# Attention on one core: where the value products and the work on the shared PSUM bank stand inside a unit

## The chip, the cores and the metric

The kernel runs on one core of a Trainium2 chip. It is one program with three stages: a feed-forward block, an attention block, a second feed-forward block. The metric is the time of one execution in microseconds of device time, as the median of several runs. The change touches only the order of work in the attention stage.

## What is computed

The input has 16 batches of 512 rows of 128 numbers. A row is first passed through a feed-forward block (a mixture of experts plus a shared part), then through attention with 16 heads of 8 numbers, then through the feed-forward block again, each on a normalised input and with a residual. The attention part is the one that matters here:

```python
x = x + 0.5 * _L0_ffn_ref(_layernorm(x, axis=-1), ...)
x = x + _L0_attn_ref(_layernorm(x, axis=-1), ...)
x = x + 0.5 * _L0_ffn_ref(_layernorm(x, axis=-1), ...)

def _L0_attn_ref(x, Wq, bq, Wk, bk, Wv, bv, Wo, bo, head_mask):
    q = (x @ Wq.T + bq).reshape(b, s, HEADS, HEAD_DIM)
    k = (x @ Wk.T + bk).reshape(b, s, HEADS, HEAD_DIM)
    v = (x @ Wv.T + bv).reshape(b, s, HEADS, HEAD_DIM)
    attn = jnp.einsum('bqhd,bkhd->bhqk', q, k) / np.sqrt(HEAD_DIM).astype(np.float32)
    attn = jax.nn.softmax(attn, axis=-1)
    attn = attn * head_mask[None, :, None, None]
    out = jnp.einsum('bhqk,bkhd->bqhd', attn, v).reshape(b, s, HIDDEN)
    return out @ Wo.T + bo
```

## The kernel before

`attention` handles the 16 batches one after another. A batch is 16 **units** (u = 0 to 15): four groups of four heads (a "quad") times four tiles of 128 keys. A unit has two halves, each for two heads of its quad. In a half TensorE (PE) makes two things, each into a bank pair of a ring of three (`p_score`):

- `score_exp`, line 927, two matmuls: the scores of this unit, from which ScalarE (ACT) makes the exponentials (line 1096);
- `score_max`, line 941, two matmuls: the scores, the other way round, of the unit 8 units ahead, of which VectorE (DVE) takes the row maxima (line 1259).

I call them E0 and M0 for the first half and E1 and M1 for the second. The ring of three sets who waits for whom (`bank_free`): an M writes into the bank pair of the E one half earlier, so it waits until ACT has read that E; an E writes into the pair of the M two halves earlier, so it waits for DVE.

`times_values` (line 958) multiplies the exponentials of a unit with the values: four matmuls, which the trace shows as eight records, each on 32 of the array's columns, into the bank `p_o`. One tile of keys after another is summed there, and after every fourth unit ACT copies `p_o` out (`copy_o`, line 1102).

All other TensorE work of the attention goes through one more PSUM bank, `p_x`. I call each such step a **piece**. There are 14 in a batch, named in `X_USES`: the transposed maxima `m0` to `m3` (line 967), which a DMA then puts beside the queries before the quad's first E may run; the transposed outputs `o0` to `o3` (975); `norm` (982), `out` (988) and `v` (915); `x` (901); and `q` and `k` (907 to 909) of the batch after the next. Every piece fills `p_x` and waits until ACT or DVE has emptied it of the piece before (`x_bank_drained`).

The order of each engine's instructions is written by hand, in the functions `batch` and `pieces` of each engine. TensorE's order in a unit before the change is E0, M0, the unit's piece, E1, M1, value products of the unit before. In units 0 and 15 there is no piece. The engines run down their own lists and meet only at semaphores.

Of the kernel before, what the change touches and what calls it, by code (L numbers as in the profile page):

```python
# [101 lines left out]
def every_batch(eng, batch):  # L102

    for k in range(NB):
        batch(Turn(0, k), k == 0, k == NB - 1)
# [637 lines left out]
def attention(nc, w, src, dst):  # L743


    UNITS = NQ * NT
# [6 lines left out]
    with ExitStack() as ctx:  # L753
# [44 lines left out]
        def there(b, n=0):  # L798

            return not isinstance(b.j, int) or b.k + n < NB  # L800
# [93 lines left out]
        def _(pe):  # L894
# [97 lines left out]
            def batch(b, is_first, is_last):  # L992
                a, c = b.step(-1), b.step(1)
                for u in range(UNITS):
                    if u % NT == 0:
                        g = u // NT
                        pe.wait_ge(max_packed[g % 2], b.count(MAX_DMA * NQ // 2, MAX_DMA * (g // 2 + 1)))
                    ahead, v = (b, u + AHEAD) if u + AHEAD < UNITS else (c, u + AHEAD - UNITS)
                    if v == 0 and there(ahead):
                        pe.wait_ge(packed[ahead.par], ahead.half(PACK_DMA, PACK_DMA))  # L1000
                    for half in range(2):
                        score_exp(b, u, half)
                        if there(ahead):
                            score_max(ahead, v, half)
                        if half == 0:
                            pieces(b, u, is_first)
                        elif u > 0:
                            times_values(b, u - 1)
                        elif not is_first:
                            times_values(a, UNITS - 1)  # L1010

            def pieces(b, u, is_first):
                a, c, e = b.step(-1), b.step(1), b.step(2)
                if u == 1:
                    turn_max(b, 1, uses(b, "m1"))
                if not is_first:
                    if u == 2:
                        turn_o(a, 3, uses(b, "o3"))
                    if u == 3:
                        turn_norm(uses(b, "norm"))  # L1020
                    if u == 4:
                        project_out(uses(b, "out"))
                if u == 5:
                    turn_max(b, 2, uses(b, "m2"))
                if u == 6:
                    turn_o(b, 0, uses(b, "o0"))
                if u == 7 and there(c):
                    project_v(uses(b, "v"))
                if u == 8 and there(e):
                    turn_x(e, uses(b, "x"))  # L1030
                if u == 9:
                    turn_max(b, 3, uses(b, "m3"))
                if u == 10:
                    turn_o(b, 1, uses(b, "o1"))
                if u == 11 and there(e):
                    project_qk(e, w.wq, uses(b, "q"))
                if u == 12 and there(e):
                    project_qk(e, w.wk, uses(b, "k"))
                if u == 13 and there(c):
                    turn_max(c, 0, uses(b, "m0"))  # L1040
                if u == 14:
                    turn_o(b, 2, uses(b, "o2"))

            begin, end = Turn(0, 0), Turn(0, NB - 1)
# [20 lines left out]
        def _(act):  # L1065
# [48 lines left out]
            def pieces(b, u, half, is_first):  # L1114
                a, c, e = b.step(-1), b.step(1), b.step(2)
                now = (u, half)
                if now == (1, 0) and not is_first:
                    copy_o(a, 3, uses(a, "o1") + 1)
                if now == (1, 1):
                    copy_max(b, 1, uses(b, "m1"))  # L1120
                if now == (3, 1) and not is_first:
# [3 lines left out]
                if now == (5, 1):  # L1125
                    copy_max(b, 2, uses(b, "m2"))
                if now == (8, 1) and there(e):
                    x_copy(e, uses(b, "x"))
                if now == (9, 0):
                    copy_o(b, 1, 0 if is_first else uses(b, "o3") + 1)  # L1130
                if now == (9, 1):
                    copy_max(b, 3, uses(b, "m3"))
                if now == (10, 0) and there(e):
                    x_high(e, uses(b, "x"))
                if now == (11, 1) and there(e):
                    operand(e, "q", w.bq, uses(b, "q"))
                if now == (12, 0) and there(e):
                    operand_high(e, "q", uses(b, "q"))
                if now == (12, 1) and there(e):
                    operand(e, "k", w.bk, uses(b, "k"))  # L1140
                if now == (13, 0):
                    copy_o(b, 2, uses(b, "o0") + 1)
                if now == (13, 1) and there(c):
                    copy_max(c, 0, uses(b, "m0"))
                if now == (14, 0) and there(e):
                    operand_high(e, "k", uses(b, "k"))

            begin, end = Turn(0, 0), Turn(0, NB - 1)
            for n in range(2):
# [96 lines left out]
        def _(dve):  # L1246
# [49 lines left out]
            def pieces(b, now, is_first):  # L1296
                a, c, e = b.step(-1), b.step(1), b.step(2)
                if there(e):
                    if now == (2, 0):
                        norm_stats(e)  # L1300
                    if now == (3, 0):
                        norm_var(e)
                if not is_first:
                    if now == (2, 1):
                        normalise(a, NQ - 1, uses(b, "o3"))
                    if now == (4, 1):
# [3 lines left out]
                if now == (7, 1) and there(c):  # L1310
                    copy_values(c, uses(b, "v"))
                if now == (10, 1):
                    normalise(b, 1, uses(b, "o1"))
                if now == (14, 1):
                    normalise(b, 2, uses(b, "o2"))

            begin, end = Turn(0, 0), Turn(0, NB - 1)
# [83 lines left out]
```

## Time and profile before

| What | Value |
|---|---|
| Time, median of 3 runs | 2092.17 us (2088.86 to 2097.89) |
| The profiled execution | 2100.33 us, of it the span of the trace 2098.1 us |
| Busy share of the span | PE 89%, DVE 71%, ACT 59%, POOL 42% |
| First feed-forward block and start of attention | 0 to 647.4 us |
| First 15 batches of attention | 647.4 to 1471.1 us |
| Last batch of attention | 1471.1 to about 1520 us |
| Second feed-forward block | to 2098.1 us |
| Mean granted clock of TensorE, as a share of 2.4 GHz | 0.93 |

The trace is one execution. Times in it count from the start of the span, and the granted clock of a stretch is a mean: 1.00 is 2.4 GHz throughout, 0.50 is 1.2 GHz throughout.

### The profile page before, as it was taken

Reading aid. Unit: us, or ns where it says so; the run is one execution under the profiler, and the core shown is the slowest. Engines: PE = TensorE matmul, PEld = TensorE weight load, DVE = VectorE, ACT = ScalarE, POOL = GpSimd, SP = SyncE. Lnnn points to the kernel's source line nnn. Section 1 sums busy time; section 2 is a strip of 40 time slices with the busy share of each in tenths; the row PEclk is TensorE's granted clock in tenths of the full one; section 3 lists DMA queues with packets and bytes.
Section 4 is the critical chain, followed back from the end, with each engine's and each line's share of the span. In section 5 each row is a group of like instructions: output and inputs, shape, how many; then the busy total and the mean of one; then the engine's idle time right before and its main releaser. Section 6 shows DMA issues by size and latency. Waiting matters only on the chain. (4 is left out here: it accounts for less than half of the span.)

```text
span 2098.1 us, 30450 instructions
## 1 busy us (share of the span) xinstructions
PE 1860.1 (89%) x9600; PEld 1108.9 (53%) x9600; DVE 1496.2 (71%) x2379; ACT 1232.2 (59%) x1914; POOL 887.4 (42%) x875
## 2 busy tenths in 40 slices
PE   3999999999937898999999988888859999999999
PEld 2777777777812333333333333333247777777777
DVE  4767777687517878777787777887447768776775
ACT  3566455555513767666676667776635565556654
POOL 2566555655621222222222222221125565556655
PEclk9999999999955989888888889998879999999999
DMA  2000000000032323222223223222010000000000
GB/s 91 21 11 31 27 24 30 10 30 10 16 59 33 47 47 47 47 42 39 41 44 44 41 41 40 53 44 35 12 36 21 31 11 31 20 30 10 30 14 16
DMA packets 43167, 68.57 MB, mean 33 GB/s; under 512 B 9916, under 2 KB 11444, under 8 KB 43060
## 3 DMA queue, kind: packets, MB, share of 16 engines
q1 hardware_dynamic: 38256, 65.15, 15.7%
q0 software_dynamic: 4096, 1.08, 0.3%
q8 instruction: 58, 0.95, 0.2%
q10 hardware_dynamic: 708, 0.98, 0.1%
q14 instruction: 49, 0.40, 0.1%
HBM read 28.36 MB, written 12.58 MB: 20 GB/s over the span
## 5 line engine op out<-in xcount | busy, mean ns | idle before, releaser
L1259 DVE TENSOR_REDUCE attn_neg_max<-attn_p_score 128x2 f32<-128x1024 f32 x512 | 624.8, 1223 | 211.2 <-PE attn_p_score L941 209.1
L572 POOL TENSOR_TENSOR ffn_hid_low<-ffn_hidden,ffn_hid_high 128x512 fp32r<-128x512 f32 x448 | 580.6, 1298 | 454.9 <-ACT ffn_hid_high L512 454.2
L1096 ACT ACTIVATE attn_exps<-attn_p_score 128x1024 f32<-128x1024 f32 x512 | 519.8, 1025 | 286.6 <-PE attn_p_score L927 284.6
L512 ACT ACTIVATE ffn_hid_high<-ffn_hidden 128x512 fp32r<-128x512 f32 x448 | 281.0, 627 | 255.7 <-DVE ffn_hidden L705 254.8
L503 ACT ACTIVATE ffn_silu<-ffn_p_gate 128x512 f32<-128x512 f32 x448 | 264.0, 589 | 207.8 <-PE ffn_p_gate L375 207.5
L698 DVE TENSOR_TENSOR ffn_gated<-ffn_silu,ffn_p_up 128x512 f32<-128x512 f32 x352 | 240.6, 684 | 175.1 <-PE ffn_p_up L375 112.2
L941 PE MATMUL attn_p_score<-k_pack,q_pack 24*128 24x512 f32 x1024 | 283.2, 553 | 57.7 <-ACT attn_exps L1096 33.0
L958 PE MATMUL attn_p_o<-attn_exps,values 128*32 128x512 f32 x2048 | 312.0, 684 | 8.4 <-ACT attn_o_raw L1102 3.3
L927 PE MATMUL attn_p_score<-q_pack,k_pack 26*128 26x512 f32 x1024 | 271.2, 539 | 14.9 <-DMA q_pack<-attn_max_rows 14.6
L927 PEld LDWEIGHTS attn_p_score<-q_pack,k_pack 26*128 26x128 f32 x1024 | 101.4, 198 | 314.7 <-issue 207.5
L705 DVE TENSOR_TENSOR ffn_hidden<-ffn_gated,ffn_p_spread 128x512 f32<-128x512 f32 x352 | 241.2, 685 | 14.9 <-PE ffn_p_spread L416 4.1
L373 PE MATMUL ffn_p_y<-ffn_hid_high,down_high 128*128 128x512 f32 x448 | 186.3, 416 | 34.0 <-POOL ffn_hid_low L572 33.3
L373 PE MATMUL ffn_p_gate<-ffn_xt_high,gate_high 128*128 128x512 f32 x448 | 188.5, 421 | 0.0
L1203 POOL DMA_DIRECT2D q_pack<-attn_max_rows x128 | 74.3, 582 | 265.0 <-ACT attn_max_rows L1090 265.0
L373 PE MATMUL ffn_p_up<-ffn_xt_high,up_high 128*128 128x512 f32 x448 | 180.4, 403 | 2.9 <-DVE ffn_gated L698 2.8
L375 PE MATMUL ffn_p_up<-ffn_xt_low,up_high 128*128 128x512 f32 x448 | 177.5, 396 | 0.0
L375 PE MATMUL ffn_p_gate<-ffn_xt_low,gate_high 128*128 128x512 f32 x448 | 177.2, 396 | 0.0
L375 PE MATMUL ffn_p_y<-ffn_hid_low,down_high 128*128 128x512 f32 x448 | 177.1, 395 | 0.0
L374 PE MATMUL ffn_p_gate<-ffn_xt_high,gate_low 128*128 128x512 f32 x448 | 176.7, 394 | 0.0
L374 PE MATMUL ffn_p_up<-ffn_xt_high,up_low 128*128 128x512 f32 x448 | 176.2, 393 | 0.0
L374 PE MATMUL ffn_p_y<-ffn_hid_high,down_low 128*128 128x512 f32 x448 | 175.4, 391 | 0.0
L941 PEld LDWEIGHTS attn_p_score<-k_pack,q_pack 24*128 24x128 f32 x1024 | 103.9, 201 | 114.9 <-ACT attn_exps L1096 90.6
(146 smaller groups left out, 2220.9 us busy)
## 6 DMA issues: line engine op xcount, KB each, us to landing
q_pack<-attn_q_high SPq DMA_DIRECT2D x128, 64.0 KB
k_pack<-attn_k_high SPq DMA_DIRECT2D x128, 64.0 KB
ffn_x_in<-in_x SPq DMA_DIRECT2D x16, 256.0 KB, 2.8
ffn_x_res<-in_x SPq DMA_DIRECT2D x16, 256.0 KB, 2.8
after_ffn<-ffn_x_out SPq DMA_DIRECT2D x16, 256.0 KB, 2.0
attn_x_in<-after_ffn SPq DMA_DIRECT2D x16, 256.0 KB, 4.6
k_pack<-attn_k_low SPq DMA_DIRECT2D x64, 64.0 KB
q_pack<-attn_q_low SPq DMA_DIRECT2D x64, 64.0 KB
```

Source lines behind the costliest of these rows:

```text
L373: nc.tensor.matmul(out, weights[0], high, start=start, stop=False)
L374: nc.tensor.matmul(out, weights[1], high, start=False, stop=False)
L375: return nc.tensor.matmul(out, weights[0], low, start=False, stop=stop)
L503: nc.scalar.activation(silu[f % 2][0:n, :], p_gate[f % 2][0:n, :], ACT.Silu).then_inc(silu_ready, 1)
L512: nc.scalar.activation(hid_high[s][0:n, :], hidden[s][0:n, :], ACT.Copy).then_inc(high_ready, 1)
L572: nc.gpsimd.tensor_tensor(hid_low[s][0:n, :], hidden[s][0:n, :], hid_high[s][0:n, :].bitcast(F32), ALU.subtract).then_inc(low_ready, 1)
L705: V.tensor_tensor(hidden[slot(b, f)][:], gated[f % 2][:], p_spread[:], ALU.mult).then_inc(weighted_ready, 1)
L927: last = nc.tensor.matmul(score_bank("exp", b, n)[:, i, :], pack["k"][b.par][rows, g, t * P:(t + 1) * P], pack["q"][b.par][rows, g, :], st ...
L941: last = nc.tensor.matmul(score_bank("max", b, n)[:, j % 2, :], pack["q"][b.par][rows, g, t * P:(t + 1) * P], pack["k"][b.par][rows, g, :] ...
L958: last = nc.tensor.matmul(p_o[h * COLS:(h + 1) * COLS, :], values[b.par][:, t, g * QUAD + h, :], exps[(2 * u + h // 2) % len(exps)][:, h % ...
L1096: nc.scalar.activation(exps[n % len(exps)][:], score_bank("exp", b, n)[:], ACT.Exp, scale=inv_sqrt)\
L1259: V.tensor_reduce(neg_max[g % 2][:, j:j + 2, t], score_bank("max", b, n)[:], AX.X, ALU.max, negate=True).then_inc(max_read, 1)
```

## The change

On TensorE the value products of two units now stand together. At the end of each even unit u come those of units u-2 and u-1, sixteen records in a row; at the end of an odd unit there are none. The piece, which stood between the two halves, now stands after everything else of a unit, and each piece comes one unit number earlier: the piece of unit 5 before is now that of unit 4. ACT's and DVE's steps on `p_x` and `p_o` are moved to match, mostly to the first half of the unit after the piece. Nothing is added or taken away.

```diff
                         score_exp(b, u, half)
                         if there(ahead):
                             score_max(ahead, v, half)
-                        if half == 0:
-                            pieces(b, u, is_first)
-                        elif u > 0:
-                            times_values(b, u - 1)
-                        elif not is_first:
-                            times_values(a, UNITS - 1)
+                    if u % 2 == 0:
+                        for back in (2, 1):
+                            if u > 0:
+                                times_values(b, u - back)
+                            elif not is_first:
+                                times_values(a, UNITS - back)
+                    pieces(b, u, is_first)
...
-                if u == 1:
+                if u == 0:
                     turn_max(b, 1, uses(b, "m1"))
...
-                if u == 5:
-                    turn_max(b, 2, uses(b, "m2"))
-                if u == 6:
+                if u == 5:
                     turn_o(b, 0, uses(b, "o0"))
...
             every_batch(pe, batch)
+            times_values(end, UNITS - 2)
             times_values(end, UNITS - 1)
...
-                if now == (1, 0) and not is_first:
-                    copy_o(a, 3, uses(a, "o1") + 1)
-                if now == (1, 1):
+                if now == (1, 0):
+                    if not is_first:
+                        copy_o(a, 3, uses(a, "o1") + 1)
                     copy_max(b, 1, uses(b, "m1"))
...
-                if now == (6, 1):
+                if now == (6, 0):
                     normalise(b, 0, uses(b, "o0"))
```

On TensorE, in a batch in the middle, from unit 3 into unit 5. Before:

```order
L927 MATMUL attn_p_score<-q_pack,k_pack 128x512 x2
L941 MATMUL attn_p_score<-k_pack,q_pack 128x512 x2
L982 MATMUL attn_p_x<-ident,attn_o_norm 128x128 x4
L927 MATMUL attn_p_score<-q_pack,k_pack 128x512 x2
L941 MATMUL attn_p_score<-k_pack,q_pack 128x512 x2
L958 MATMUL attn_p_o<-attn_exps,values 32x512 x4
L927 MATMUL attn_p_score<-q_pack,k_pack 128x512 x2
L941 MATMUL attn_p_score<-k_pack,q_pack 128x512 x2
L988 MATMUL attn_p_x<-wo,attn_ot 128x128 x4
```

TensorE again, the same place after the change, units 3 and 4:

```order
L927 MATMUL attn_p_score<-q_pack,k_pack 128x512 x2
L941 MATMUL attn_p_score<-k_pack,q_pack 128x512 x2
L927 MATMUL attn_p_score<-q_pack,k_pack 128x512 x2
L941 MATMUL attn_p_score<-k_pack,q_pack 128x512 x2
L988 MATMUL attn_p_x<-wo,attn_ot 128x128 x4
L927 MATMUL attn_p_score<-q_pack,k_pack 128x512 x2
L941 MATMUL attn_p_score<-k_pack,q_pack 128x512 x2
L927 MATMUL attn_p_score<-q_pack,k_pack 128x512 x2
L941 MATMUL attn_p_score<-k_pack,q_pack 128x512 x2
L958 MATMUL attn_p_o<-attn_exps,values 32x512 x8
L967 MATMUL attn_p_x<-ident,attn_max_parts 32x128
```

The piece is gone from between the halves; E0, M0, E1 and M1 follow each other in every unit, and the value products come every second unit, eight matmuls at a time.

On ScalarE, units 5 and 6 of such a batch. Before:

```order
L1102 ACTIVATE attn_o_raw<-attn_p_o 128x512
L1096 ACTIVATE attn_exps<-attn_p_score 128x1024
L1090 ACTIVATE attn_max_rows<-attn_p_x 32x128
L1096 ACTIVATE attn_exps<-attn_p_score 128x1024 x6
L1069 ACTIVATE attn_xt<-attn_p_x 128x512
```

ScalarE after the change, the same place:

```order
L1104 ACTIVATE attn_o_raw<-attn_p_o 128x512
L1092 ACTIVATE attn_max_rows<-attn_p_x 32x128
L1098 ACTIVATE attn_exps<-attn_p_score 128x1024 x6
L1071 ACTIVATE attn_xt<-attn_p_x 128x512
```

The two copies now stand together between the exponentials of unit 5's first and second half.

## Rows read from the trace of the kernel before

**Rows 1.** Busy time by stretch: microseconds, busy time (and records) of each engine, clock, DMA:

```profile
647.40:1471.10 823.70, 736.80 (x4556) 275.45 (x4556) 642.76 (x781) 561.74 (x697) 210.43 (x337) 0.89 0.27 42
1471.10:1520.00 48.90, 42.93 (x259) 14.51 (x255) 22.43 (x26) 33.32 (x40) 6.02 (x13) 0.83 0.02 8
...
1312.60:1363.70 51.10, 44.64 (x310) 17.22 (x306) 42.96 (x54) 37.72 (x47) 14.53 (x23) 1.00 0.28 49
```

**Rows 2.** TensorE in order of time, units 14 and 15: start, length, line, count, idle before:

```profile
1027.10 0.50 PE L927 MATMUL attn_p_score<-q_pack,k_pack 26*128 26x512 f32 x2
...
1027.54 0.66 PE L975 MATMUL attn_p_x<-ident,attn_o_raw 128*128 128x128 f32 x4
1028.12 0.50 PE L927 MATMUL attn_p_score<-q_pack,k_pack 26*128 26x512 f32 x2
1028.72 0.50 PE L941 MATMUL attn_p_score<-k_pack,q_pack 24*128 24x512 f32 x2
1029.15 1.06 PE L958 MATMUL attn_p_o<-attn_exps,values 128*32 128x512 f32 x8
1030.15 0.50 PE L927 MATMUL attn_p_score<-q_pack,k_pack 26*128 26x512 f32 x2
...
1030.54 0.50 PE L927 MATMUL attn_p_score<-q_pack,k_pack 26*128 26x512 f32 x2
1031.76 0.52 PE L941 MATMUL attn_p_score<-k_pack,q_pack 24*128 24x512 f32 x2 [0.72 <-ACT attn_exps L1096]
```

**Rows 3.** ScalarE in order of time, the exponentials of unit 15:

```profile
1030.69 1.94 ACT L1096 ACTIVATE attn_exps<-attn_p_score 128x1024 f32<-128x1024 f32 x2 [0.59 <-PE attn_p_score L927]
```

**Rows 4.** TensorE in order of time, the same batch boundary at the lower clock:

```profile
1032.21 1.94 PE L958 MATMUL attn_p_o<-attn_exps,values 128*32 128x512 f32 x8
1034.08 0.79 PE L927 MATMUL attn_p_score<-q_pack,k_pack 26*128 26x512 f32 x2
...
1035.99 0.79 PE L941 MATMUL attn_p_score<-k_pack,q_pack 24*128 24x512 f32 x2 [0.69 <-ACT attn_exps L1096]
1036.71 1.93 PE L958 MATMUL attn_p_o<-attn_exps,values 128*32 128x512 f32 x8
1038.58 0.79 PE L927 MATMUL attn_p_score<-q_pack,k_pack 26*128 26x512 f32 x2
```

**Rows 5.** Busy time by stretch around a fall and a rise of the clock:

```profile
1030.50:1032.10 1.60, 0.88 (x8) 0.37 (x4) 1.56 (x3) 1.41 (x2) 0.05 (x1) 1.00 0.02 5
1032.10:1049.10 17.00, 16.24 (x71) 4.99 (x69) 10.36 (x15) 7.75 (x10) 1.58 (x4) 0.50 0.57 80
1161.80:1165.20 3.40, 3.40 (x20) 2.01 (x20) 1.90 (x2) 1.69 (x2) 1.01 (x3) 0.50 0.54 63
1165.20:1169.00 3.80, 3.30 (x29) 0.94 (x21) 3.40 (x4) 2.76 (x5) 1.27 (x1) 1.00 0.78 140
```

**Rows 6.** Pieces on TensorE in order of time, at the upper clock:

```profile
1018.40 0.47 PE L907 MATMUL attn_p_x<-attn_xt_high,wq_high 128*128 128x512 f32 x1 [0.47 <-DVE attn_o_norm L1277]
...
1018.94 0.39 PE L909 MATMUL attn_p_x<-attn_xt_low,wq_high 128*128 128x512 f32 x1
...
1024.71 0.27 PE L967 MATMUL attn_p_x<-ident,attn_max_parts 128*32 128x128 f32 x1 [0.17 <-ACT attn_k_full L1079]
...
1488.23 1.16 PE L988 MATMUL attn_p_x<-wo,attn_ot 128*128 128x128 f32 x8
```

**Rows 7.** Pieces on TensorE in order of time, at the lower clock:

```profile
1039.31 0.40 PE L967 MATMUL attn_p_x<-ident,attn_max_parts 128*32 128x128 f32 x1
...
1043.81 1.11 PE L975 MATMUL attn_p_x<-ident,attn_o_raw 128*128 128x128 f32 x4
...
1161.54 2.08 PE L988 MATMUL attn_p_x<-wo,attn_ot 128*128 128x128 f32 x8
```

**Rows 8.** Waits between 650 and 1500 us: total, times, longest:

```profile
PE attn_p_score L927 <- DMA q_pack<-attn_max_rows: 11.2, 7, 3.2
```

More of the change, by code:

```diff
@@ L1019, in pieces @@
                     if u == 3:
-                        turn_norm(uses(b, "norm"))
-                    if u == 4:
                         project_out(uses(b, "out"))
+                if u == 4:
+                    turn_max(b, 2, uses(b, "m2"))
                 if u == 5:
-                    turn_max(b, 2, uses(b, "m2"))
-                if u == 6:
                     turn_o(b, 0, uses(b, "o0"))
-                if u == 7 and there(c):
+                if u == 6 and there(c):
                     project_v(uses(b, "v"))
-                if u == 8 and there(e):
+                if u == 7 and there(e):
@@ L1030, in pieces @@
                     turn_x(e, uses(b, "x"))
+                if u == 8:
+                    turn_max(b, 3, uses(b, "m3"))
                 if u == 9:
-                    turn_max(b, 3, uses(b, "m3"))
-                if u == 10:
                     turn_o(b, 1, uses(b, "o1"))
+                if u == 10 and there(e):
+                    project_qk(e, w.wq, uses(b, "q"))
                 if u == 11 and there(e):
-                    project_qk(e, w.wq, uses(b, "q"))
-                if u == 12 and there(e):
@@ L1038, in pieces @@
                     project_qk(e, w.wk, uses(b, "k"))
-                if u == 13 and there(c):
+                if u == 12 and there(c):
                     turn_max(c, 0, uses(b, "m0"))
-                if u == 14:
+                if u == 13:
                     turn_o(b, 2, uses(b, "o2"))
@@ L1116, in pieces @@
                 now = (u, half)
-                if now == (1, 0) and not is_first:
-                    copy_o(a, 3, uses(a, "o1") + 1)
-                if now == (1, 1):
+                if now == (1, 0):
+                    if not is_first:
+                        copy_o(a, 3, uses(a, "o1") + 1)
                     copy_max(b, 1, uses(b, "m1"))
-                if now == (3, 1) and not is_first:
+                if now == (3, 0) and not is_first:
                     copy_ot(uses(b, "norm"))
@@ L1124, in pieces @@
                     copy_o(b, 0, 0 if is_first else uses(a, "o2") + 1)
[L1125 removed]
                     copy_max(b, 2, uses(b, "m2"))
+                if now == (8, 0) and there(e):
+                    x_copy(e, uses(b, "x"))
                 if now == (8, 1) and there(e):
[L1128 removed]
+                    x_high(e, uses(b, "x"))
                 if now == (9, 0):
                     copy_o(b, 1, 0 if is_first else uses(b, "o3") + 1)
[L1131 removed]
                     copy_max(b, 3, uses(b, "m3"))
[L1133 to L1134 removed]
+                if now == (11, 0) and there(e):
+                    operand(e, "q", w.bq, uses(b, "q"))
                 if now == (11, 1) and there(e):
[L1136 removed]
+                    operand_high(e, "q", uses(b, "q"))
                 if now == (12, 0) and there(e):
[L1138 removed]
+                    operand(e, "k", w.bk, uses(b, "k"))
                 if now == (12, 1) and there(e):
[L1140 removed]
+                    operand_high(e, "k", uses(b, "k"))
                 if now == (13, 0):
                     copy_o(b, 2, uses(b, "o0") + 1)
[L1143 to L1146, printed above, removed]
+                    if there(c):
+                        copy_max(c, 0, uses(b, "m0"))
             begin, end = Turn(0, 0), Turn(0, NB - 1)
@@ L1298, in pieces @@
                 if there(e):
-                    if now == (2, 0):
+                    if now == (1, 0):
                         norm_stats(e)
-                    if now == (3, 0):
+                    if now == (2, 1):
                         norm_var(e)
                 if not is_first:
-                    if now == (2, 1):
+                    if now == (2, 0):
                         normalise(a, NQ - 1, uses(b, "o3"))
-                    if now == (4, 1):
+                    if now == (4, 0):
                         residual(a, uses(b, "out"))
-                if now == (6, 1):
+                if now == (6, 0):
                     normalise(b, 0, uses(b, "o0"))
-                if now == (7, 1) and there(c):
+                if now == (7, 0) and there(c):
                     copy_values(c, uses(b, "v"))
-                if now == (10, 1):
+                if now == (10, 0):
                     normalise(b, 1, uses(b, "o1"))
-                if now == (14, 1):
+                if now == (14, 0):
                     normalise(b, 2, uses(b, "o2"))
```

4 lines of the change are left out of this document (3 added, 1 removed).

## The prediction, made before the changed kernel had run

> **What bounds the kernel now.** I read the busy time by stretch first, since the change touches only the attention. The first 15 batches take 823.7 us, 54.9 us each, and the last one 48.9 us. TensorE is busy 736.8 of the 823.7 us, more than DVE (642.8) or ACT (561.7), and its mean granted clock there is 0.89. One batch, from 1312.6 to 1363.7 us, ran at 1.00 throughout and took 51.1 us [rows 1]. So two things make up a batch: TensorE's own order of work, and the time it spends at its lower clock.
>
> Then I read TensorE in order of time. Unit 14 has a piece. It starts at 1027.10; the piece (the output transposes) runs from 1027.54 to 1028.12; E1 follows, M1 starts at 1028.72, the value products at 1029.15, and the next unit at 1030.15: 3.05 us. Unit 15 has no piece. It starts at 1030.15, E1 stands at 1030.54, and then TensorE idles 0.72 us until M1 at 1031.76, released by ACT [rows 2]. The reason stands in ACT's rows: the exponential of E0 starts at 1030.69, and two together take 1.94 us, so the first leaves at about 1031.7 [rows 3]. M1 needs that bank pair. **M1 comes 1.61 us after E0 whether or not there is a piece between them.** That is the cover under which pieces run today. At the lower clock the same distance is 1035.99 - 1034.08 = 1.91 us [rows 4].
>
> **The change at the upper clock.** With the piece behind M1 a unit is, to the start of the next thing, 1.61 (E0 to M1) + 0.43 (M1) + 1.00 (value products, here as half of a double block) = 3.04 us [rows 2], and the piece comes on top. Sixteen units are 48.6 us. Pieces, from start to the next score (a row's length less 0.07, as 1027.54 + 0.66 against 1028.12): turning maxima 0.20; four transposes 0.59; `out` and `v` 1.09 each; `q` and `k` 0.86 each, from 1018.40 to 1018.94 + 0.39 [rows 2, 6]. A batch has 4, 6, 2 and 2 of these: 0.80 + 3.54 + 2.18 + 1.72 = 8.2 us. Together 56.9 us, against 51.1 for the batch of before at that clock. The unit's end gives them no cover: TensorE runs in order and nobody else is late there.
>
> **The same at the lower clock.** A unit is 1.91 + 0.72 (M1 to the value products) + 1.87 (value products, 1036.71 to 1038.58) = 4.50 us [rows 4], sixteen are 72.0. Pieces: 0.33, 1.04, 2.01 [rows 7], and for `q` and `k`, which no row shows at this clock in a steady batch, between 0.86 and twice that, 1.72; I take 1.55, 0.86 scaled as the transposes are (1.04 to 0.59). Sum 1.32 + 6.24 + 4.02 + 3.10 = 14.7. A batch is 86.7 us.
>
> **Which clock.** The falls of before show when it goes. After the 1.6 us of units 14 and 15 in which TensorE was busy 0.88, without any piece, the clock stood at 0.50 for 17 us [rows 5]. Unit 15 before that fall had eight records of value products, the scores, one wait of 0.72 and no piece. In the steady batches the falls come in units 15 and 0, the two without a piece, or where TensorE waits for a DMA in front of unit 4. The rises are the other way round: from 1161.8 to 1165.2 us TensorE was busy all 3.40 us, most of it with the projection of `out` (2.08 us, full array, [rows 7]) and value products, and after it the clock was 1.00 [rows 5]. Fully busy stretches of mostly scores did not lift it: the 17 us at 0.50 were 16.24 busy.
>
> The changed order makes both happen in every pair of units. Between two blocks of value products stand the piece, the scores of an odd unit with their wait, a second piece and the scores of an even unit with their wait: at the upper clock 0.59 + 2.04 + 0.59 + 2.04 = 5.3 us with no value products in them and two waits of 0.7, leaner than units 15 and 0 were. So I expect the clock to fall there. Then come sixteen records of value products and a piece without a wait, 3.74 + 1.04 = 4.8 us at the lower clock, denser than what lifted the clock before. So I expect it to rise behind them, too late for the block itself. **The clock is low in the even unit, the block and its piece, and high in the odd unit.** Per pair: scores of the even unit 1.91 + 0.72 = 2.63; block 2 x 1.87 = 3.74; scores of the odd unit 1.61 + 0.43 = 2.04; 8.41 us, eight pairs 67.3. Pieces after even units (four times 0.33, `norm` 1.04, `v` 2.01, `q` 1.55) 5.9; after odd ones (five times 0.59, `out` 1.09, `k` 0.86) 4.9. A batch is 78.1 us.
>
> The Trainium skill says otherwise ("TensorE: Matmul & The Clock Gate", section "Why this matters for your kernels"): it ties a throttled clock to pauses between bursts of matmuls several times longer than any here. By that rule the clock would stay up. The trace speaks against it, since the clock fell behind a wait of 0.72 us; I keep it as the third case below.
>
> **Smaller terms.** The wait of E for the maxima's DMA, 11.2 us in seven [rows 8], goes: the piece `m1` comes a unit earlier and the units are longer. It is in the 54.9 of before and not in my 78.1. The two ACT copies that now stand together delay the exponential of an odd unit's second half, and so M0 of the next unit, by up to 0.6 us, four times a batch. But the following M1 has to wait 1.61 us after E0 anyway, and swallows it. I take 0; if it didn't, up to 1.2 us a batch, 18 in all. DVE's steps are moved by half a unit; DVE has 22% of the stretch free [rows 1], 0. Changes between score matmuls, value products and full-array work fall from eight to five per pair. What one costs is bounded by the value block: 1.00 us at the upper clock where half of 1.87 is 0.935, so 0.065 at most from that side, 24 times a batch 1.6 us, 25 in all; below, nothing. I take 0, since most of it is hidden behind running matmuls.
>
> "TensorEngine Tiling (Array Packing)" in the Trainium skill, section "Key Properties", says that a change of tiling mode drains TensorE, which speaks for this change. It gives no price; with the bound just worked out the sum would be 25 us lower.
>
> **The sum.** 78.1 - 54.9 = 23.2 us for 15 batches, 348. The last batch has look-ahead scores only in its first half: half of 23.2 there, 12, and nothing in the second half. Together 360 us. The profiled execution took 2100.3, so its like would take 2460; it stood 8 us above the median of the runs, and 2092 + 360 gives **2452 us**.
>
> **Rivals.**
>
> *Lower clock throughout.* If the blocks don't lift the clock (no row shows sixteen records in a row), a batch is 86.7: 31.8 x 15 + 16 = 493, 2585 us. For it: fully busy stretches that didn't lift it. Against it: those were mostly scores.
>
> *Lower clock for a third.* If it falls more rarely, say every second or third pair, a batch is 56.9 + 29.8 / 3 = 66.8: 11.9 x 15 + 6 = 185, 2277 us. For it: one whole batch of before kept 1.00 [rows 1]. Against it: that batch had cover for its pieces.
>
> *Upper clock throughout, and slightly slower.* 56.9 - 54.9 = 2.0 x 15 + 1 = 31, 2123 us; with the 25 of the mode changes 2098.
>
> *Faster.* The denser blocks keep the clock up, and a mode change costs more than my bound. The batch then gives back 54.9 - 51.1 = 3.8 us of low clock and loses 5.8 to uncovered pieces. It breaks even at 2.0 / 24 = 0.083 us per change saved. At 0.15 a batch is 1.6 us shorter, 2092 - 24 = 2068 us. Against it: the clock fell at a leaner density of waits than the new order has.
>
> **Chances.** Alternating clock 66%; lower throughout 14%; a third 12%; upper throughout 8%, of it 3 faster, 2 the same, 3 slower. I call "the same" a time within 0.5% of 2092, about what a measurement here can tell. The range reaches from the case of a third to that of the lower clock throughout: 2280 to 2590. The likeliest case alone would lie between 2400 and 2500. Faster 0.03, same 0.02, slower 0.95.
>
> **What would show it.** In the trace of the changed kernel, M1 1.6 us behind E0 at the upper and 1.9 at the lower clock in every unit, with TensorE idle about 0.7 before it, released by ACT: right. M1 earlier than that: my first step is wrong. Sixteen records of value products that take 3.7 us, with scores of the odd unit 0.5 us long: alternating clock, mean granted clock in the attention about 0.64 (low for 8 x 6.37 + 5.9 = 56.9 of 78.1 us). A mean near 0.5 or 0.95 is one of the rivals. Pieces with idle time before them, waiting for the bank, or E waiting for the maxima's DMA, would be a term that I left out. The feed-forward stages should keep their time.

## The result, and the profile after

The changed kernel took 2423.76 us (median of 4 runs, 2418.72 to 2424.01), the kernel before 2095.03 us with them. The ratio is 1.157, with a 95% interval of 1.153 to 1.160: 329 us slower. Ratios here leave out executions that took over 1.5% longer than the fastest of the same kernel. The forecast was 360 us slower, 2452 us, with a range of 2280 to 2590.

The busy time by stretch of the changed kernel (microseconds, then busy time and records of PE, weight loads, DVE, ACT and POOL, then clock and DMA), to be read against [rows 1]:

```profile
648.30:1784.80 1136.50, 959.32 (x4550) 348.77 (x4550) 641.45 (x780) 556.59 (x697) 210.25 (x337) 0.67 0.19 31
...
1254.80:1330.30 75.50, 63.50 (x308) 23.34 (x308) 43.00 (x53) 37.41 (x48) 14.51 (x23) 0.68 0.22 33
1176.80:1254.80 78.00, 66.17 (x308) 23.88 (x308) 43.14 (x53) 37.38 (x48) 14.51 (x23) 0.65 0.20 32
```

The first 15 batches grew from 823.7 to 1136.5 us, from 54.9 to 75.8 us each. DVE and ACT did the same work as before (642 and 557 us). The mean granted clock went from 0.89 to 0.67; since the trace has only the two levels 1.00 and 0.50, that is a share of 2 x (1 - 0.67) = 66% of the stretch at 1.2 GHz; before it was 22%. The feed-forward stages kept their time.

TensorE in order of time in the changed kernel, end of unit 4 to unit 8 of a batch (start, length, line, count, idle before), to be read against [rows 2, 4]:

```profile
1276.56 1.92 PE L958 MATMUL attn_p_o<-attn_exps,values 128*32 128x512 f32 x16
...
1278.63 0.50 PE L927 MATMUL attn_p_score<-q_pack,k_pack 26*128 26x512 f32 x2
...
1278.97 0.40 PE L927 MATMUL attn_p_score<-q_pack,k_pack 26*128 26x512 f32 x2
1280.24 0.50 PE L941 MATMUL attn_p_score<-k_pack,q_pack 24*128 24x512 f32 x2 [0.87 <-ACT attn_exps L1098]
1280.96 0.63 PE L975 MATMUL attn_p_x<-ident,attn_o_raw 128*128 128x128 f32 x4 [0.22 <-ACT attn_max_rows L1092]
1281.52 0.56 PE L927 MATMUL attn_p_score<-q_pack,k_pack 26*128 26x512 f32 x2
...
1283.19 0.79 PE L941 MATMUL attn_p_score<-k_pack,q_pack 24*128 24x512 f32 x2 [0.21 <-ACT attn_exps L1098]
1283.91 3.64 PE L958 MATMUL attn_p_o<-attn_exps,values 128*32 128x512 f32 x16
1287.48 1.70 PE L915 MATMUL attn_p_x<-wv,attn_xt 128*128 128x128 f32 x8
1289.12 0.49 PE L927 MATMUL attn_p_score<-q_pack,k_pack 26*128 26x512 f32 x2
...
1290.73 0.50 PE L941 MATMUL attn_p_score<-k_pack,q_pack 24*128 24x512 f32 x2 [0.87 <-ACT attn_exps L1098]
1291.57 0.68 PE L901 MATMUL attn_p_x<-ident,attn_xn 128*128 128x128 f32 x4 [0.35 <-DVE values L1265]
1292.18 0.79 PE L927 MATMUL attn_p_score<-q_pack,k_pack 26*128 26x512 f32 x2
...
1294.10 0.79 PE L941 MATMUL attn_p_score<-k_pack,q_pack 24*128 24x512 f32 x2 [0.60 <-ACT attn_exps L1098]
1294.82 3.64 PE L958 MATMUL attn_p_o<-attn_exps,values 128*32 128x512 f32 x16
```

Read the lengths. In unit 5 a pair of scores takes 0.50 us, so the clock is up; TensorE waits 0.87 us for ACT in front of M1, then runs the piece in the open. In unit 6 the scores turn to 0.79 us in mid-unit, and the sixteen records of value products take 3.57 us (1283.91 to 1287.48), at the lower clock. Behind them, in unit 7, the scores are back at 0.5. In unit 8 the low clock is there from the first score. The same in windows over that stretch:

```profile
1283.90:1287.40 3.50, 3.50 (x18) 0.60 (x16) 1.50 (x3) 0.15 (x1) 0.00 (x0) 0.50 0.00 0
1287.40:1289.10 1.70, 1.70 (x12) 1.51 (x8) 0.00 (x0) 0.00 (x0) 0.00 (x0) 0.63 0.00 0
1289.10:1292.10 3.00, 1.78 (x13) 0.91 (x12) 2.41 (x3) 1.94 (x2) 0.00 (x0) 0.99 0.00 0
1292.10:1298.70 6.60, 6.00 (x27) 1.56 (x25) 3.00 (x3) 2.94 (x4) 0.43 (x2) 0.50 0.01 2
```

TensorE's clock is low where it is busy all the time and high where it is busy 1.78 of 3.00 us: in this stretch the upper clock arrives when the dense work is over.

### The profile page after: what moved, and what is told of

It is laid out like the page before. It is cut to its first block and busy times, and to the rows that moved or that the text cites. A ratio compares the mean times of both kernels' runs of the same rounds, so it can differ in the third digit from the quotient of the medians.

```text
span 2421.8 us, 30419 instructions
## 1 busy us (share of the span) xinstructions
PE 2087.0 (86%) x9569; PEld 1184.4 (49%) x9600; DVE 1496.1 (62%) x2379; ACT 1227.2 (51%) x1914; POOL 887.4 (37%) x875
## 5 line engine op out<-in xcount | busy, mean ns | idle before, releaser
L1098 ACT ACTIVATE attn_exps<-attn_p_score 128x1024 f32<-128x1024 f32 x512 | 511.8, 1021 | 613.8 <-PE attn_p_score L927 611.6
L941 PE MATMUL attn_p_score<-k_pack,q_pack 24*128 24x512 f32 x1024 | 329.0, 643 | 170.5 <-ACT attn_exps L1098 153.9
L958 PE MATMUL attn_p_o<-attn_exps,values 128*32 128x512 f32 x2048 | 443.8, 1014 | 1.0 <-ACT attn_exps L1098 1.0
L927 PE MATMUL attn_p_score<-q_pack,k_pack 26*128 26x512 f32 x1024 | 260.8, 567 | 12.8 <-DVE attn_neg_max L1259 8.2
L941 PEld LDWEIGHTS attn_p_score<-k_pack,q_pack 24*128 24x128 f32 x1024 | 119.8, 232 | 298.6 <-ACT attn_exps L1098 271.8
L1194 POOL TENSOR_TENSOR attn_max_parts<-attn_neg_max,zeros 128x16 fp32r<-128x16 f32 x64 | 13.9, 218 | 494.7 <-DVE attn_neg_max L1259 494.7
L958 PEld LDWEIGHTS attn_p_o<-attn_exps,values 128*32 128x32 f32 x2048 | 73.7, 153 | 212.5 <-issue 145.1
```

The source lines that it names most:

```text
L927: last = nc.tensor.matmul(score_bank("exp", b, n)[:, i, :], pack["k"][b.par][rows, g, t * P:(t + 1) * P], pack["q"][b.par][rows, g, :], st ...
L941: last = nc.tensor.matmul(score_bank("max", b, n)[:, j % 2, :], pack["q"][b.par][rows, g, t * P:(t + 1) * P], pack["k"][b.par][rows, g, :] ...
L958: last = nc.tensor.matmul(p_o[h * COLS:(h + 1) * COLS, :], values[b.par][:, t, g * QUAD + h, :], exps[(2 * u + h // 2) % len(exps)][:, h % ...
L1098: nc.scalar.activation(exps[n % len(exps)][:], score_bank("exp", b, n)[:], ACT.Exp, scale=inv_sqrt)\
```

## The experiments

The theory (A) has two parts. The pieces lost their cover, the wait for M1; and the clock falls between the double blocks of value products and rises behind them. Its rivals put all of the loss on the first part (B), on the idle gap in each unit (C, I), or on the spacing of value products alone (E). Each run is compared with the kernel before on its own chip, whose median was between 2094 and 2101 us.

### Half of the change each

**Value products in pairs, pieces as before.**

```diff
                         if half == 0:
                             pieces(b, u, is_first)
-                        elif u > 0:
-                            times_values(b, u - 1)
-                        elif not is_first:
-                            times_values(a, UNITS - 1)
+                        elif u % 2 == 0:
+                            for back in (2, 1):
+                                if u > 0:
+                                    times_values(b, u - back)
+                                elif not is_first:
+                                    times_values(a, UNITS - back)
...
             every_batch(pe, batch)
+            times_values(end, UNITS - 2)
             times_values(end, UNITS - 1)
```

> The value products of two units stand together at each even unit's end, as in the changed kernel; the pieces keep their place between the two halves, as before. Theory A (two costs: uncovered pieces, and a clock that falls in the units without value products and rises behind each double block): the pieces are covered again, but the clock still alternates, so a batch falls from 75.8 us to about 8 x 8.4 + the overhang of the long pieces = 68 to 70 us, 2300 us in all, and the mean granted clock of the attention stays near 0.70. Rival B (all of the loss is the lost cover under M1): about 2095 us, as before, at a clock near 0.89.

Measured: 2249.78 us, ratio 1.070 (1.062 to 1.078), 149 us slower. Busy time by stretch, its first 15 batches:

```profile
647.90:1615.70 967.80, 847.09 (x4548) 319.86 (x4549) 642.20 (x780) 559.79 (x697) 210.32 (x337) 0.76 0.22 36
```

With every piece back under the wait the clock still alternates: 0.76, so 48% of the stretch is low. B is out. A batch takes 64.5 us, less than the 68 to 70 that I expected: 37 of the 128 double blocks took 1.85 us, all at the upper clock, and 38 took 3.57, against 11 and 111 in the changed kernel.

**Pieces at the end, value products of one unit in every unit.**

```diff
-                    if u % 2 == 0:
-                        for back in (2, 1):
-                            if u > 0:
-                                times_values(b, u - back)
-                            elif not is_first:
-                                times_values(a, UNITS - back)
+                    if u > 0:
+                        times_values(b, u - 1)
+                    elif not is_first:
+                        times_values(a, UNITS - 1)
                     pieces(b, u, is_first)
...
             every_batch(pe, batch)
-            times_values(end, UNITS - 2)
             times_values(end, UNITS - 1)
```

> The pieces and all copies stand where the changed kernel has them; the value products of one unit stand in each unit's end, as before, ahead of the piece. Theory A: every unit has its eight value records again, so the clock is up most of the time; a batch is 56.9 us at the upper clock and some 2 to 5 us more for low stretches around the two units without a piece, 57 to 62 us, 2130 to 2210 us in all, clock 0.88 or more. Rival B (all of the loss is the lost cover): near 2424 us. Rival C (the clock falls because each unit now has an idle wait of 0.7 us, wherever the value products stand): clock near 0.67 and 2400 us or more.

Measured: 2172.59 us, ratio 1.035 (1.025 to 1.044), 72 us slower. Busy time by stretch, the first 15 batches and one whole batch at the upper clock, and behind it two rows of TensorE:

```profile
647.30:1551.40 904.10, 700.76 (x4559) 258.47 (x4560) 643.36 (x781) 553.60 (x697) 210.58 (x337) 0.92 0.25 39
892.20:949.80 57.60, 43.72 (x310) 16.63 (x307) 43.05 (x54) 37.18 (x47) 14.53 (x23) 1.00 0.25 43
```

```profile
1085.96 0.50 PE L941 MATMUL attn_p_score<-k_pack,q_pack 24*128 24x512 f32 x2 [0.87 <-ACT attn_exps L1095]
...
1089.22 0.50 PE L941 MATMUL attn_p_score<-k_pack,q_pack 24*128 24x512 f32 x2 [0.79 <-ACT attn_exps L1095]
```

The second fence is TensorE in order of time, M1 of two units in a row: every unit now has a wait of 0.8 to 0.9 us before M1, and TensorE is busy 700.76 of 904.1 us (78%), less than in the changed kernel (84%; part of that is only that the same matmuls last longer at the lower clock). Yet the clock is at 0.92. So C is out: idle gaps of this size don't take the clock down where every unit has its value products. The batch at 1.00 takes 57.6 us; the lost cover costs 57.6 - 51.1 [rows 1] = 6.5 us a batch at equal clock.

The two halves cost 149 and 72 us, together 221, and the whole change 329. The missing 108 us are the two acting on each other, and most of it by the clock: by length and mean clock the 15 batches spend about 180 us at the lower clock before, 465 and 145 in the two halves, and 750 in the changed kernel, some 320 more than the halves add up to. My reading is that the wait which the pieces no longer fill makes the stretch between the blocks emptier, and that a piece in the open costs about twice as much at the lower clock ([rows 6, 7]: 1.16 and 2.08 us for eight records). No run separates these two.

### Work added to the changed kernel

**Four, then eight, useless transposes in each unit's wait.** They go into the bank pair that E1 overwrites right behind them.

```diff
+            def filler(b, u, times):
+                bank_free(pe, "exp", b, 2 * u + 1)
+                for n in range(times):
+                    for t in range(NT):
+                        nc.tensor.transpose(score_bank("exp", b, 2 * u + 1)[:, n % 2, t * P:(t + 1) * P], w.ident[:], w.ident[:])
...
                         if there(ahead):
                             score_max(ahead, v, half)
+                        if half == 0:
+                            filler(b, u, 1)
```

> The changed kernel with useless work added: in every unit, between M0 and E1, four transposes of the identity into the bank pair that E1 overwrites right behind. E1 then starts at 1.0 instead of 0.4 us, still ahead of M1 at 1.6, so the filler itself is covered by the wait. Theory A (the low clock between the double blocks is the larger cost): the clock is up much more of the time, a batch goes from 75.8 to 58 to 64 us, 2150 to 2230 us in all, though work is added. Rival E (the clock follows the spacing of the value products alone, and filler does not count): 2424 us or slightly more, clock 0.67 in the attention.

> As the run before, with eight transposes, so that E1 starts at 1.5 us, still ahead of M1. Theory A: if four left some low stretches, eight leave next to none: the changed order at the upper clock, 57 to 59 us a batch, 2130 to 2160 us. That is what the uncovered pieces cost by themselves. Rival E: 2424 us or more.

Measured: 2192.14 us with four, ratio 1.047 (1.039 to 1.055), and 2169.42 us with eight, ratio 1.035 (1.028 to 1.041). Busy time by stretch, the 15 batches and one of them, with four and then with eight:

```profile
647.00:1558.50 911.50, 866.14 (x5508) 387.54 (x5508) 640.78 (x780) 565.09 (x697) 211.27 (x337) 0.94 0.24 38
1132.40:1190.50 58.10, 55.13 (x372) 25.54 (x371) 42.94 (x53) 38.03 (x48) 14.58 (x23) 1.00 0.29 43
```

```profile
647.50:1534.90 887.40, 854.13 (x6468) 471.05 (x6469) 642.96 (x780) 566.54 (x696) 210.94 (x337) 0.99 0.25 39
...
1003.90:1063.10 59.20, 57.05 (x438) 31.47 (x435) 43.09 (x53) 38.11 (x47) 14.56 (x23) 1.00 0.29 42
```

The run with eight settles it. The order of the changed kernel is untouched, 1920 transposes are added to its first 15 batches, and it is 254 us faster. The clock stays at 1.00 from the second of these batches to the last. E is out. Of the 329 us that the change costs, at least 254 go with the clock. The 75 that remain are not the price of the order alone: the kernel before also spent 22% of its attention at the lower clock, and the filler has a price of its own. At equal clock a batch takes 51.1 us before, 58.1 with four transposes and 59.2 with eight; by the 1.1 us between the last two I estimate 57 without any, 6 us a batch for the order.

**Score matmuls as filler.** The same place in each unit; E1's own two matmuls are made three extra times.

```diff
...
+                for _ in range(3):
+                    for i in range(2):
+                        nc.tensor.matmul(score_bank("exp", b, n)[:, i, :],
+                                         pack["k"][b.par][rows, g, t * P:(t + 1) * P],
+                                         pack["q"][b.par][rows, g, :], start=True, stop=True,
+                                         tile_position=((2 + i) * ROWS, 0))
```

> The changed kernel again with filler between M0 and E1 in every unit, but of the other kind: E1's own two score matmuls (32 of the array's rows each) are made three extra times, about 1.0 us, and overwritten. TensorE is then as busy in the wait as with eight full-array transposes. Rival I (what keeps the clock up is that TensorE does not idle): 2150 to 2190 us and a clock of the attention near 0.99, as with the eight transposes. Theory A2 (score matmuls count for less than full-array work and value products): the clock still alternates, 0.70 to 0.85, and the time lies between 2250 and 2430 us.

Measured: 2269.31 us (median of 4, 2214.8 to 2287.35). Busy time by stretch, of an execution of 2264 us, and behind it the filler of one unit and the E1 that follows:

```profile
647.00:1632.00 985.00, 925.79 (x6033) 429.65 (x6033) 646.82 (x785) 566.57 (x701) 211.49 (x341) 0.87 0.22 36
```

```profile
1108.39 0.86 PE L999 MATMUL attn_p_score<-q_pack,k_pack 26*128 26x512 f32 x6
1109.09 0.39 PE L927 MATMUL attn_p_score<-q_pack,k_pack 26*128 26x512 f32 x2
```

TensorE is busy 925.79 of 985.0 us, 94%, and the clock is at 0.87, against 0.99 with the transposes and 0.92 in the run that was busy only 78%. So I is out, too: it isn't idleness as such. The six filler matmuls took 0.70 us (1108.39 to 1109.09), not the 1.0 expected, so the fair comparison is with four transposes, 0.58 us: TensorE was then busy 866.14 of 911.5 us, 95%, and the clock was 0.94. Score matmuls helped, but less than full-array transposes over no more time. The median lies in the range of A2, the clock a little above it; even the fastest of the four, 2214.8 us, is slower than every run with transposes and outside the range of rival I. How much each kind counts was not measured one by one.

### The kernel before: can its own low stretches be had?

The same reasoning says that the kernel before loses time at its two empty units, 0 and 15. Seven runs followed it.

**Filler in units 0 and 15** (four transposes of the identity into `p_x` once it is drained).

> The kernel before, with useless work added: in the two units of a batch without a piece (0 and 15) four transposes of the identity into the shared bank, which nobody reads, between the two halves. Theory A: the filler is covered by the wait for M1 and keeps the clock up there, so the low stretches of 3.8 us worth a batch go: 2095 - 16 x 3.8 = about 2035 us, mean clock of the attention 0.97 or more. Rival C (the clock falls by the idle gap itself or for another reason): 2095 us or slightly more, the low stretches stay.

Measured: 2089.92 us, ratio 0.992 (0.987 to 0.996). The medians are 11 us apart, about 0.5%, far from the 60 us expected. Its profiled execution took 2101 us, more than its median. TensorE in order of time, between units 3 and 4 of a batch, and then at the start of its unit 8:

```profile
1045.26 1.07 PE L958 MATMUL attn_p_o<-attn_exps,values 128*32 128x512 f32 x8
1048.07 0.50 PE L927 MATMUL attn_p_score<-q_pack,k_pack 26*128 26x512 f32 x2 [1.74 <-DMA q_pack<-attn_max_rows]
...
1063.47 0.50 PE L927 MATMUL attn_p_score<-q_pack,k_pack 26*128 26x512 f32 x2 [2.64 <-DMA q_pack<-attn_max_rows]
...
1064.59 0.79 PE L927 MATMUL attn_p_score<-q_pack,k_pack 26*128 26x512 f32 x2
```

The falls in units 0 and 15 are gone, and batches that no longer lose time there run into the DMA of the maxima in front of units 4 and 8 and wait. Behind many of these waits the clock falls: here behind the 2.64 us, where the scores turn from 0.50 to 0.79 us. It doesn't behind all: it stayed up after the 1.74 us. The gain was given back later.

**Value products in the wait of units 0 and 15**, and nothing added.

```diff
                         score_exp(b, u, half)
+                        cover = half == 1 and u in (0, UNITS - 1)
+                        if cover and u > 0:
+                            times_values(b, u - 1)
+                        elif cover and not is_first:
+                            times_values(a, UNITS - 1)
                         if there(ahead):
                             score_max(ahead, v, half)
...
```

> The kernel before; only in units 0 and 15, which have no piece, the value products stand between E1 and M1, in the wait, instead of behind M1. Nothing is added. Theory A: each such unit gets about 0.7 us shorter (the wait of 0.72 us is filled) and the clock stays up, 15 x (1.5 + 3.8) = 80 us, 2015 us in all. Rival D (M1 comes later, so its row maxima come later, and the next unit's E1 waits for VectorE): the unit keeps its 3.0 us; the clock may still stay up, 2040 us; if it doesn't, 2095.

Measured: 2094.4 us, ratio 0.994 (0.990 to 0.998). Part of rival D came true; TensorE in units 15 and 0:

```profile
967.65 0.50 PE L927 MATMUL attn_p_score<-q_pack,k_pack 26*128 26x512 f32 x2
...
969.81 0.44 PE L927 MATMUL attn_p_score<-q_pack,k_pack 26*128 26x512 f32 x2
...
971.29 0.50 PE L927 MATMUL attn_p_score<-q_pack,k_pack 26*128 26x512 f32 x2 [0.61 <-DVE attn_neg_max L1262]
```

Unit 15 shrank to 969.81 - 967.65 = 2.16 us, but its late M1 makes the next unit's E1 wait 0.61 us for DVE, and the DMA waits in front of unit 4 are there as before. The mean clock of the stretch stays at 0.89.

**`m1` earlier, and all pieces up to `m2` earlier.** In the first, `m1` stands in unit 0 and the value products fill units 1 and 15; in the second, `m1` to `m2` are all one unit earlier.

> The kernel before with three moves: the piece m1 stands in unit 0, between E1 and M1, and ScalarE copies it there (its DMA starts 3 us earlier); in units 1 and 15, now without a piece, the value products stand between E1 and M1. Theory F (with the two empty units filled, what still pulls the clock down is the wait of unit 4's first score for the DMA of the maxima, 0.7 to 3.4 us): that wait goes, and a batch takes 49 to 51 us, 2015 to 2040 us in all, clock of the attention above 0.95. Rival G (the DMA lands late because the queue is full of other transfers, however early it is issued): the wait stays, about 2090 us.

> The kernel before with all pieces from m1 to m2 one unit earlier (m1 behind M1 of unit 0, o3, norm and out in units 1 to 3 between the halves, m2 in unit 4 between E1 and M1), the copies with them, and the value products of units 0 and 15 between E1 and M1. Theory F: both DMAs of maxima (in front of units 4 and 8) start 3 us earlier, no wait is left; 49 to 51 us a batch, 2010 to 2040 us. Against it: unit 5 is now without a piece and may let the clock fall (rival: 2060 to 2095 us).

Measured: 2097.49 us, ratio 1.004 (1.000 to 1.008), and 2112.07 us, ratio 1.009 (1.005 to 1.012). The DMA wait is gone, as expected, and neither is faster: other waits took its place. Waits of TensorE in the second, and the clock:

```profile
PE attn_p_x L967 <- POOL attn_max_parts L1206: 22.4, 15, 2.1
```

```profile
646.70:1481.10 834.40, 751.60 (x4556) 284.19 (x4558) 639.48 (x780) 567.86 (x697) 209.79 (x337) 0.86 0.26 42
```

**Filler in units 0, 15 and in front of units 4 and 8; then the shifted order with filler; then that with earlier statistics.** The last differs from the one before it by two lines:

```diff
-                    if now == (2, 0):
+                    if now == (1, 0):
                         norm_stats(e)
-                    if now == (3, 0):
+                    if now == (2, 0):
                         norm_var(e)
```

> The kernel before, with useless transposes of the identity into the bank pair that the next E overwrites: four in units 0 and 15 between M0 and E1, and eight in front of the first score of units 4 and 8, where TensorE sometimes waits for the DMA of the maxima. Theory H (the gain of the earlier filler run was given back because the DMA waits in front of units 4 and 8 became the next places at which the clock falls): with these filled too the low stretches go, 51 us a batch, 2030 to 2045 us in all, clock of the attention above 0.97. The eight transposes cost up to 1.1 us each where there is no wait. Rival: a wait longer than the filler still lets the clock fall, 2070 to 2095 us.

> The order of the shifted run (m1 in unit 0, o3, norm, out in units 1 to 3, m2 in unit 4, so that no score waits for a DMA), with the value products behind M1 in every unit and four useless transposes of the identity between M0 and E1 in the units without a piece there (0, 4, 5, 15). Theory H: neither an empty unit nor a DMA wait is left, so the clock stays up; 49.5 to 50.5 us a batch, 2010 to 2030 us in all. Rival: m1 or m2 waits for GpSimd's split of the maxima by more than 1 us, and the clock falls there, 2060 to 2095 us.

> The run before (shifted order with filler), with VectorE's statistics of the batch after the next one unit earlier (units 1 and 2). There GpSimd's split of the maxima stood behind the normalisation, m2 waited up to 1.5 us for it in unit 4, and the clock fell in that same unit in 13 of 15 batches. Theory H (any wait of over a microsecond in a unit takes the clock down, for several units): the split now comes in time, the fall goes, 49.5 to 50.5 us a batch, 2010 to 2030 us in all. Rival: the clock falls in unit 4 or 5 all the same, 2100 to 2140 us.

Measured: 2083.97 us, ratio 0.992 (0.989 to 0.995); 2137.91 us, ratio 1.015 (1.009 to 1.021); 2067.32 us, ratio 0.988 (0.982 to 0.995). Busy time by stretch, in the same order:

```profile
647.30:1448.90 801.60, 726.42 (x4916) 294.08 (x4916) 643.39 (x781) 565.88 (x697) 210.50 (x337) 0.98 0.28 43
```

```profile
647.30:1503.00 855.70, 787.05 (x4798) 308.88 (x4799) 643.16 (x781) 570.81 (x697) 209.45 (x339) 0.86 0.26 41
```

```profile
647.10:1444.40 797.30, 731.18 (x4797) 288.47 (x4798) 641.75 (x781) 567.97 (x697) 211.07 (x337) 0.95 0.28 44
```

In the first the clock stays up (0.98), but filler where no wait is costs time of its own and the DMA waits remain: 53.4 us a batch. In the second one long wait was left, in unit 4, where `m2` waited for GpSimd, which normalised the rows of the batch after the next first:

```profile
1113.33 0.50 PE L927 MATMUL attn_p_score<-q_pack,k_pack 26*128 26x512 f32 x2
1115.32 0.39 PE L967 MATMUL attn_p_x<-ident,attn_max_parts 128*32 128x128 f32 x1 [1.49 <-POOL attn_max_parts L1215]
1115.64 0.79 PE L941 MATMUL attn_p_score<-k_pack,q_pack 24*128 24x512 f32 x2
```

The scores turn from 0.50 to 0.79 us across that one wait of 1.49 us, and the batch from about 51 to 58. Two steps of DVE one unit earlier took it away: from a ratio of 1.015 to one of 0.988, for two lines. This last kernel is 1.2% faster than the kernel before and the fastest one found. It falls short of the 2010 to 2030 us expected, since a DMA wait of up to 2.3 us in front of unit 8 is left, which takes the clock down in some batches.

## Why the prediction was right, point by point

**M1 stands 1.61 us behind E0, with or without a piece: right.** 1278.63 to 1280.24 at the upper clock, 1292.18 to 1294.10 = 1.92 at the lower, ACT the releaser both times. TensorE idled 0.87 and 0.60 us before it.

**Uncovered pieces at the upper clock, 56.9 us a batch: right.** Measured were 57.6 with single value blocks, and 58.1 and 59.2 with double ones and four and eight transposes, which gives my 57 without them. In it two errors cancel: the value blocks are cheaper than I took them (below), and I left out small waits: the two copies that ACT makes in a row delay not only the next M0, which the wait for M1 did swallow (1281.52 to 1283.19 is 1.67 us), but also the output transposes, which wait 0.22 us for the second copy. `x` waits 0.35 us for DVE.

**Alternating clock: right, and in most of the places named.** Low in the even unit and its block, high in the odd unit. The mean clock was forecast at 0.64 and came out at 0.67. The places differ in three ways. Unit 15, which has no piece, I had at the upper clock; it ran at the lower in every steady batch and took 2.51 us (1252.32 to 1254.83), where I had 2.04:

```profile
1252.32 0.79 PE L927 MATMUL attn_p_score<-q_pack,k_pack 26*128 26x512 f32 x2
...
1254.23 0.79 PE L941 MATMUL attn_p_score<-k_pack,q_pack 24*128 24x512 f32 x2 [0.69 <-ACT attn_exps L1098]
1254.83 0.63 PE L927 MATMUL attn_p_score<-q_pack,k_pack 26*128 26x512 f32 x2
```

The piece `v` ran partly at the upper clock, 1.64 us (1287.48 to 1289.12) for my 2.01. And in two of each three batches the block of unit 4 ran at the upper clock (the row of 1.92 us at 1276.56, first above); the batch of 75.5 us above (0.68) is of that kind, the one of 78.0 us (0.65) is not. I had taken every pair as equal. That the 78.0 equals my 78.1 is partly luck: the cheaper value blocks and `v` took off what unit 15 and the small waits put on.

**The value block: mis-sized.** I took twice a single block, 3.74 us at the lower clock and 2.00 at the upper. It was 3.57, and in the filler runs 1.85 (1184.43 to 1186.28 in the one with eight):

```profile
1184.43 1.92 PE L958 MATMUL attn_p_o<-attn_exps,values 128*32 128x512 f32 x16
1186.28 0.28 PE L967 MATMUL attn_p_x<-ident,attn_max_parts 128*32 128x128 f32 x1
```

So two blocks joined save 0.15 to 0.17 us, 8 times a batch 1.3 us, 20 us in 15 batches. Joining two blocks takes out two changes of mode, so if the changes are the cause, one is worth about 0.08 us. My bound was 0.065 each, 1.6 us a batch; it was nearly right, and the miss was to take nothing of it, as hidden behind running matmuls. "TensorEngine Tiling (Array Packing)" in the Trainium skill, section "Key Properties", says that a mode change drains the engine. The trace agrees in that a joined block, with two changes of mode fewer, is 0.15 us shorter or more; that it is the drain and not another cost of starting a block, no run shows. The gain that the change was good for was there, about a sixteenth of what it cost.

**The DMA wait goes: right.** Where [rows 8] has seven waits, the waits of TensorE in the changed kernel have none after the first score of the stage. **The last batch: right.** Forecast 12 us longer; the rest of the span outside the 15 batches grew by 323.7 - 312.8 = 10.9.

**The sum.** 23.2 us a batch were forecast and 20.9 measured. The 2.3 us between them are the cheaper value blocks (1.3), the blocks of unit 4 at the upper clock (2.5 in two of three batches, 1.7) and shorter first and fifteenth batches (71.1 and 72.5 us, 0.6 in the mean), less the small waits left out (0.22 us four times and 0.35 once, 1.2); unit 15 and `v` about cancel. By my own scaling `q` and `k` at the lower clock were 1.52, not 1.55, which changes nothing.

**The rivals.** Upper clock throughout did not happen. The run with eight transposes, 2169 us, bounds its price from above; my 2123 rested on 56.9 us a batch, which the estimate of 57 bears out. The clock did fall behind waits of under a microsecond. The Trainium skill ("TensorE: Matmul & The Clock Gate", section "Why this matters for your kernels") ties it to longer pauses between bursts. For this order, with no wait over 0.9 us in the steady batches, that rule gave the wrong side, by 250 us or more.

## What to carry to other kernels

Work that stands in front of a wait that ends anyway is free, and behind it is not; before moving it, look for the wait that it covers. And look at what TensorE runs between its dense blocks: grouping dense work may leave the rest so thin that the clock falls there and comes back only behind the next block, which then runs at half speed. Where a clock loss is suspected, useless full-array matmuls in an existing wait test it in one run: if the granted clock rises and the kernel gets faster by added work, it was the clock.

## What the runs showed of the hardware

- TensorE's granted clock does not follow how busy the trace shows it. Busy 78% with value products in every unit: 0.92. Busy 84% with value products in every second unit: 0.67. Busy 94% with score matmuls as filler: 0.87. Busy 95% with four transposes: 0.94. The same matmul counts as busy for longer at the lower clock, so these shares are not shares of work.
- Across a single wait of 1.49 us, with filler in the units around it, the clock went to 0.50, and such a batch took 58 us, where one at the upper clock takes 51. Across a wait of 1.74 us, in the kernel before with filler in units 0 and 15, it stayed at 1.00. The length of a wait alone doesn't tell.
- The pattern repeats: the changed kernel's batches take 78.0, 75.5 and 75.2 us in turn from the second to the fourteenth.
- Joining two blocks of column-tiled matmuls into one of sixteen records saved 0.15 us at the upper clock.
